# A graph-attention kernel whose rounds finish the last batch's softmax, weighing and sums ahead of the new batch's rows

## What is computed

```python
q, k, v = projections of the nodes                      # [3125, 8, 16]
e = edge_attr @ We                                      # second layer only, 64 -> 128
logits = sum(q[dst] * (k[src] + e), -1) / 4             # [53125, 8]
m = segment_max(logits, dst); ex = exp(logits - m[dst])
alpha = ex / segment_sum(ex, dst)[dst]
agg = segment_sum(alpha[..., None] * (v[src] + e), dst) # [3125, 128]
x = residual and norms and a 128 -> 512 -> 128 gelu network of agg
```

## Time and profile before

| what | value |
| --- | --- |
| median of 3 runs | 1341.0 us (1340.02 to 1342.21) |
| the profiled execution | 1341.56 us, span 1339.8 us |
| mean granted clock of TensorE | 0.796 of full speed |
| busy share of the span | DVE 77%, POOL 75%, PE 65%, ACT 56% |
| gathers of the first layer | 52.85 to 583 us |
| gathers of the second layer | 697.5 to 1224 us |
| transfers | 280.52 MB, 209 GB/s over the span |

### The profile page before, as it was taken

One profiled execution on the slowest core, in us unless ns is written; L12 is line 12 of the kernel. 1 busy time (PEld: TensorE's weight loads), 2 busy tenths in 40 slices (PEclk: granted clock), 3 DMA queues, 4 the chain that ended last, 5 costly groups with the idle time before them and its releaser, 6 DMA issues. The chain is left out here.

```text
span 1339.8 us, 25090 instructions
## 1 busy us (share of the span) xinstructions
PE 877.0 (65%) x5107; PEld 768.1 (57%) x5107; DVE 1030.4 (77%) x2702; ACT 747.1 (56%) x2535; POOL 1001.0 (75%) x1840
## 2 busy tenths in 40 slices
PE   3535666466456565558996586676676677776784
PEld 1335555455455565557875476665565565666673
DVE  4747878778668677796665888988988888899676
ACT  3314675574664655655540464665655755656775
POOL 4688888888888888832348888888888888884254
PEclk9756777777786766778997787887887887878798
DMA  7679877677777777750147788888888888885001
GB/s 200 184 205 284 243 238 247 217 241 240 221 243 231 220 246 230 228 174 3 55 123 232 250 257 273 253 255 281 245 258 268 250 268 270 262 254 175 1 1 49
DMA packets 227727, 280.52 MB, mean 209 GB/s; under 512 B 48262, under 2 KB 176420, under 8 KB 224119
## 3 DMA queue, kind: packets, MB, share of 16 engines
q1 hardware_dynamic: 185808, 167.97, 40.2%
q0 software_dynamic: 39936, 109.11, 27.2%
q10 hardware_dynamic: 1830, 1.86, 0.6%
HBM read 239.72 MB, written 39.08 MB: 208 GB/s over the span
## 5 line engine op out<-in xcount | busy, mean ns | idle before, releaser
L548 POOL DMA_INDIRECT KV<-kv_table,idx x832 | 803.7, 966 | 167.4 <-issue 154.7
L847 PE MATMUL PS<-QW,OHT 128*128 128x128 f32 x1664 | 304.7, 342 | 170.1 <-DVE PR L1146 148.9
L847 PEld LDWEIGHTS PS<-QW,OHT 128*128 128x128 f32 x1664 | 274.0, 248 | 191.3 <-issue 187.2
L675 ACT ACTIVATE AGG<-AGG,PC,RCS x800 | 309.2, 387 | 2.2 <-ACT AGG L671 1.5
L892 PE MATMUL PS<-OH,KV 128*128 128x128 f32 x1600 | 234.2, 301 | 25.4 <-ACT AGG L675 22.4
L892 PEld LDWEIGHTS PS<-OH,KV 128*128 128x128 f32 x1600 | 218.0, 215 | 38.9 <-issue 35.7
L1146 DVE TENSOR_TENSOR PR<-KV,PS 128x512 f32<-128x512 f32 x208 | 140.4, 675 | 119.1 <-DMA KV<-kv_table,idx 117.3
L671 ACT ACTIVATE AGG<-PS 128x127 f32 x800 | 208.7, 261 | 1.0 <-issue 0.9
L1139 DVE TENSOR_TENSOR KV<-KV,PS 128x1024 f32<-128x1024 f32 x104 | 125.4, 1206 | 70.5 <-DMA KV<-kv_table,idx 58.3
L667 ACT ACTIVATE PC<-PS 128x4 f32<-128x4 f32 x200 | 33.8, 169 | 233.4 <-PE PS L892 199.1
L867 PE MATMUL PS<-ident,AL 128*128 128x128 f32 x52 | 24.4, 468 | 198.2 <-DVE AL L1233 198.2
(11 more groups left out here) (163 smaller groups left out, 1330.7 us busy)
## 6 DMA issues: line engine op xcount, KB each, us to landing
QW<-q_table SPq DMA_DIRECT2D x832, 64.0 KB
REL<-rel_dram SPq DMA_DIRECT2D x52, 512.0 KB
window_dram<-OH SPq DMA_DIRECT2D x25, 1024.0 KB
OH<-window_dram SPq DMA_DIRECT2D x50, 512.0 KB, 7.2
KV<-kv_table,idx POOLq DMA_INDIRECT x832
EA<-in_edge_batch SPq DMA_DIRECT2D x52, 256.0 KB, 3.3
kv_table<-KV SPq DMA_DIRECT2D x24, 256.0 KB, 2.2
q_table<-KV SPq DMA_DIRECT2D x24, 128.0 KB, 2.2
```

Of the source, the lines that this page charges most:

```text
L548: g.indirect_dma_start(KV[:, s, j, :], None, kv_table, bass.IndirectOffsetOnAxis(ap=idx[:, s, j:j + 1], axis=0)).then_inc(gathered[s][hh], 16)
L675: sc.activation(AGG[:, ds(at, 1)], AGG[:, ds(at, 1)], ACT.Identity, bias=PC[:, m:m + 1], scale=RCS[:, n % SLOTS, j:j + 1]).then_inc(S["act ...
L847: last = te.matmul(o, OHT[:, q // 2, e0:e0 + P], QW[:, n % 2, 4 * q + m, :], start=True, stop=True)
```

## The change

Round n now does, on every engine, softmax and weighing of batch n - 1 and its sums, and the rows of batch n. On DVE the softmax of n - 1 comes whole, then `one_hots1(n + 1)`, then the four weighings, then the rows of n without anything between them. On ACT `one_hots(n + 1)` comes last, behind the four quarters of sums of n - 1. On PE the sums' last two quarters stand behind the queries and edge parts of the second half of n. There are G + 1 rounds. SP loads or stores the windows of n one round earlier, and the numbers of `FIRST_PACE` are lower. The work itself, in instructions and bytes, is the same.

```diff
-FIRST_PACE = ((2, 3), (4, 6), (7, 8))
+FIRST_PACE = ((2, 3), (4, 4), (6, 7))
...
-            f(0, soft=False, sums=False)
-            f(1, sums=False)
-            for n in range(2, G - 1):
+            f(0, sums=False)
+            for n in range(1, G):
                 f(n)
-            f(G - 1, more=False)
-            f(G, logits=False, more=False)
-            f(G + 1, logits=False, soft=False, more=False)
+            f(G, logits=False)
...
 (SP)
+                    if n:
+                        row_gates(n)
+                    if l and n == G - 1:
+                        load_last_windows()
                     if l and n + 1 < G:
                         features(n + 1, 0)
+                    if l and n < G - 1:
+                        load_windows(n, 0)
                     if l and n + 1 < G:
                         features(n + 1, 1)
+                    if l and n < G - 1:
+                        load_windows(n, 1)
                     if n + 2 < G:
                         places(n + 2)
                         load_queries(n + 2)
+                    if l == 0:
+                        store_windows(n)
...
 (ACT)
                     if sums:
                         exponentials(n - 1)
                     if logits:
                         gates_of(n)
                     if sums:
                         scale_at_d(n - 1)
                     if n == G:
                         warm(ACT.Gelu)
+                    if sums:
+                        for q in range(4):
+                            if n == G:
+                                add_up_last(q)
+                            else:
+                                add_up(n - 1, q)
+                    if n + 1 < G:
+                        one_hots(n + 1)
...
 (PE)
                     if sums:
                         turn_logits(n - 1)
                     if logits:
+                        queries_of(n, 0)
+                        queries_of(n, 1)
+                        if l:
+                            edge_part(n, 0)
+                            edge_part(n, 1)
+                    if sums:
+                        turn_alpha(n - 1)
+                        spread_gains(n - 1)
+                        add_up(n - 1, 0)
+                        add_up(n - 1, 1)
+                    if n == G:
+                        attention(*quads[0])
+                    if logits:
                         queries_of(n, 2)
+                        if l:
+                            edge_part(n, 2)
                     if sums:
+                        add_up(n - 1, 2)
...
                     if logits:
                         queries_of(n, 3)
+                        if l:
+                            edge_part(n, 3)
                     if sums:
+                        add_up(n - 1, 3)
...
 (DVE)
+                    if sums:
+                        if l == 0 and n < G:
+                            windows(n - 1, 0)
                         forward_max(n - 1)
                         turn_max(n - 1)
                         backward_max(n - 1)
                         carry_max(n - 1)
+                        max_back(n - 1)
+                        shifts(n - 1)
+                        if l == 0 and n < G:
+                            windows(n - 1, 1)
+                        segment_sums(n - 1)
+                        turn_sums(n - 1)
+                        totals(n - 1)
+                        carry_sum(n - 1)
+                        sums_back(n - 1)
+                        alphas(n - 1)
+                        gains(n - 1)
+                        next(places, None)
+                        for q in range(4):
+                            weigh(n - 1, q)
                     if logits:
+                        add_edges(n, 0)
+                        products(n, 0)
                         add_edges(n, 1)
                         add_products(n, 0)
                         products(n, 1)
                         add_products(n, 1)
...
                         add_edges(n, 2)
                         products(n, 2)
+                        add_edges(n, 3)
                         add_products(n, 2)
                         products(n, 3)
                         add_products(n, 3)
+                    else:
+                        add_first_nodes()
```

More of the change, by code:

```diff
@@ L462, in _ @@
                     round(n)
-                if l == 0:
-                    store_windows(G - 1)
             full = N // P
@@ L709, in gates_of, with round @@
                     sc.activation(GF[:, n % SLOTS, :], FIRST[:, ds(n * P, P)], ACT.Identity, bias=minus_big[:, 0:1], scale=BIG)                        .then_inc(S["ga_ready"], 1)
-                def round(n, logits=True, soft=True, sums=True, more=True):
-                    if n == G + 1:
-                        for q in range(4):
-                            add_up_last(q)
-                        return
+                def round(n, logits=True, sums=True):
                     if sums:
-                        add_up(n - 2, 0)
-                        add_up(n - 2, 1)
-                    if soft:
                         exponentials(n - 1)
@@ L723, in round @@
                     if sums:
-                        add_up(n - 2, 2)
-                    if sums:
-                        add_up(n - 2, 3)
-                    if more:
-                        one_hots(n + 1)
-                    if soft:
                         scale_at_d(n - 1)
@@ L916, in attention, with round @@
                     last.then_inc(S["att_ready"], w)
-                def round(n, logits=True, soft=True, sums=True, more=True):
+                def round(n, logits=True, sums=True):
                     if sums:
-                        add_up(n - 2, 0)
-                    if sums:
-                        add_up(n - 2, 1)
-                    if n == G + 1:
-                        attention(*quads[0])
-                        add_up(n - 2, 2)
-                        attention(*quads[1])
-                        add_up(n - 2, 3)
-                        return
-                    if n == G:
@@ L953, in round @@
-                    if logits and n < G - 1:
-                        turn_logits(n)
-                queries_of(0, 0)
-                queries_of(0, 1)
-                if l:
-                    edge_part(0, 0)
-                    edge_part(0, 1)
+                        add_up(n - 1, 3)
                 written_out(round)
@@ L1258, in weigh, with round @@
                     v.tensor_tensor(v4, v4, at, ALU.mult).then_inc(S["pv_ready"], 1)
-                def round(n, logits=True, soft=True, sums=True, more=True):
-                    if n == G - 1:
-                        last_logits()
-                        return
-                    if n == G + 1:
-                        add_first_nodes()
-                        return
-                    if logits:
-                        add_edges(n, 0)
-                    if soft:
+                def round(n, logits=True, sums=True):
+                    places = one_hots1(n + 1) if n + 1 < G else iter(())
+                    if sums:
+                        if l == 0 and n < G:
+                            windows(n - 1, 0)
                         forward_max(n - 1)
-                    if logits:
-                        products(n, 0)
-                    if soft:
                         turn_max(n - 1)
@@ L1276, in round @@
                         carry_max(n - 1)
+                        max_back(n - 1)
[12 more added lines that the diff above has]
+                            weigh(n - 1, q)
                     if logits:
+                        add_edges(n, 0)
+                        products(n, 0)
                         add_edges(n, 1)
                         add_products(n, 0)
-                    if soft:
-                        max_back(n - 1)
-                    if logits:
                         products(n, 1)
-                    if soft:
-                        shifts(n - 1)
-                    if logits:
                         add_products(n, 1)
-                    places = one_hots1(n + 1) if more else iter(())
                     next(places, None)
+                    if l == 0 and n == G - 1:
+                        windows(n, 0)
+                        windows(n, 1)
                     if logits:
@@ L1305, in round @@
                         products(n, 3)
-                    if soft:
-                        sums_back(n - 1)
-                    if soft and l == 0 and n < G:
-                        windows(n - 1, 0)
-                    if soft:
-                        alphas(n - 1)
-                        gains(n - 1)
-                    if soft and l == 0 and n < G:
-                        windows(n - 1, 1)
-                    if logits:
-                        add_products(n, 3)
-                    if soft:
-                        for q in range(4):
-                            weigh(n - 1, q)
```

78 lines of the change are left out of this document (2 added, 76 removed).

## The result

The changed kernel takes 1364.35 us (median of 4 runs, 1363.66 to 1368.14), the kernel before 1341.61 us in the same session (4 runs, 1340.02 to 1345.07). The ratio is 1.0177 with a 95% interval of 1.0162 to 1.0193, so the change costs 22.7 us. The prediction was 1354, slower, with a range that reaches to 1385. The profiled execution took 1364.29 us.

The account below looks back on a forecast made before the run. POOL's gathers bound both layers; the second layer's loop through the places, 21.55 us, would exceed their 20.27. 1341.56 + 20.6 - 7.7 = 1354.5, so about 1354 us; range 1329 to 1385, likeliest case 1344 to 1376.

Parts of the forecast that it names:

- What bounds before: POOL's queue of gathers sets the pace of both layers, 20.4 and 20.27 us a batch.
- the other side: Rival: gathers stay the bound in the second layer, places landing in under 4.0 us or PE never late; 1327, chance 0.30.
- The loop through the places: Weighing waits for the previous weighing through ACT's one-hots, SP, the places' transfer and DVE's one-hots; 19.2 and 21.55 us.
- 13.9 + 0.1 + 4.4 + 0.8 = 19.2 us: First layer's loop: ACT, SP, transfer of places, DVE's one-hots and handover; under 20.4, so the gathers keep the pace.
- ACT's 13.9 us: First layer, weighing to end of ACT's one-hots: 2.3 until sums start plus 11.6, with 0.3 added for the address load.
- the indices wait for a landed batch anyway, which hides it: On SP, indices queued behind window stores that now wait for DVE a round later; taken to cost nothing.
- The lag of the first rounds: In the rival that the first layer falls too: DVE's early lag, some 7 us, stays and grows; 1372, chance 0.07.
- 15.4 + 0.1 + 5.25 + 0.8 = 21.55 us: Second layer's loop: ACT, SP, transfer of places, DVE's one-hots and handover; over the gathers' 20.27, likeliest case, chance 0.45.
- 4.34 + 3.7: Second layer, third quarter of sums on PE: first product done, then queries, edges and sums; put at 8.3 us.
- 20.6 - 7.7 = 12.9 us: Net loss: 20.6 us lost in the second layer, 7.7 us won behind the first layer's last gather.
- The signs that were named: Profile signs: gathers 1.27 us apart, one-hots idle for REL, weighings 21 to 22 and 20.4, POOL waiting, last weighing near 595.
- The middle between 7.2 and 3.3 us: Second layer's transfer of the places, 512 KB, taken between the windows' and the features' landings: 5.25 us.

Follow-up runs that it names:

- all_three: Changed kernel with DVE's one-hots back behind the weighing, ACT's address loads before the sums, and eight gate loads at the end of SP's round 1; 1326.79 us, ratio 0.9893.
- late_places: Changed kernel with DVE's one-hots moved back behind the weighing, into the rows of the next batch; 1346.05 us, ratio 1.0030.
- split_places: Changed kernel with the transfer of the places cut in two, so DVE's half need not wait for ACT; 1356.09 us, ratio 1.0102.
- calm_start: Changed kernel with a larger first gate load, the eight remaining in pairs over SP's rounds 2 to 5, late weights in round 7; 1356.41 us, ratio 1.0115.
- gates_spread: Changed kernel with the eight remaining gate loads split three, three and two at the ends of SP's rounds 0, 1 and 2; 1362.14 us, ratio 1.0148.
- old_pace: Changed kernel with FIRST_PACE as in the kernel before; 1368.85 us, ratio 1.0179.
- early_addresses: Changed kernel with ACT loading all 16 node offsets behind the exponential and gates, before waiting for the sums; 1343.82 us, ratio 1.0008.
- two: Changed kernel with late_places and early_addresses together, gate loads not moved; 1330.9 us, ratio 0.9911.
- store_early: Changed kernel with the first layer's window store issued by SP before the places and queries; 1405.71 us, ratio 1.0456.

## Why the prediction was right in sign and range, and where it was wrong

**What bounds before, and the other side.** Right. A reordering can win only behind the gathers; that rival's price, 1327, is what all_three measures, though with two edits that the rival did not have in mind.

**The loop through the places, as a mechanism.** Right: in the second layer opening it (late_places, split_places) takes 7.5 to 9.6 us away and the waits with it. In 14 of 22 rounds there the places are the last wait in front of the weighing, in the other 8 ACT's exponential.

**The first layer: "13.9 + 0.1 + 4.4 + 0.8 = 19.2 us, under 20.4; the gathers keep the pace."** This step failed, and the first layer lost 20.2 us instead of winning 7.7. The term that was too small is ACT's 13.9 us, which is 15.9: the sums start at 2.87, not 2.3, and from there to the end of the one-hots are 12.99 us, not 11.6, mostly because the load of the addresses, taken at 0.3, leaves 1.46 us idle under the windows' store. With 15.9 + 0.1 + 4.1 + 0.8 = 20.9 the prediction's own formula gives the measured round, but it is not this loop that mostly holds it: split_places opened it, and the round stayed at 20.84. The prediction asked for 1.2 us more to turn this layer over; it got 1.7.

**Loops that were not listed.** ACT makes its one-hots ahead of the next exponential, and 4.9 us of softmax follow it to the weighing: 15.9 + 4.9 = 20.8. At the prediction's 13.9 it would have been 18.8 and harmless, so its absence is not what failed, but it is why loosening the places alone (split_places) brings this layer nothing. The loop through SP's queries and the store of the windows was not listed either; "the indices wait for a landed batch anyway, which hides it" looks at what stands behind the store and not at DVE, which waits for it. It is 20.3 us in the changed kernel and did no harm there.

**The lag of the first rounds.** It stood in a rival, at some 7 us and a chance of 0.07. By the prediction's own steps batch 2 could be weighed at 113.7 + 1.85 + 2.6 + 0.55 + 6.3 + 0.3 = 125.3 (its last gather ends at 113.7); it was at 144.34, 19 us late. Then 21 rounds add 0.52 each, 10.9, and the last two, without one-hots to make, give 3.5 back (20.19 and 17.13 us against 2 x 20.4): 26.5 us. Measured against all_three it is 621.08 - 594.06 = 27.0. So by this reckoning about seven tenths of the distance from the gathers' bound is the old late start, which a loop over the gathers' pace can't work off, and the rest is the loop's own excess. Two runs bear on that share: calm_start, in which 8.4 of 12.0 us came through to the last weighing, and gates_spread, in which all of 2.85 did. Both are gone with a loop of 19.4 us, as all_three shows.

**The second layer: "15.4 + 0.1 + 5.25 + 0.8 = 21.55 us."** Right in kind, too long in size. Measured are 20.7. One round by the timelines of DVE, ACT, SP and DVE:

```profile
1024.09 1.28 DVE L1235 TENSOR_TENSOR KV<-KV,PS 128x512 f32<-128x512 f32 x2
...
1037.54 1.15 ACT L648 ACTIVATE OHT<-OHT,one_col 128x1024 f32<-128x1024 f32 x1
...
1038.77 0.33 SPq L351 DMA_DIRECT2D REL<-rel_dram  x1
...
1044.15 0.75 DVE L1105 TENSOR_SCALAR OHT<-REL,iota_part 128x1024 f32<-128x1024 bf16 x1 [0.86 <-DMA REL<-rel_dram]
1044.82 1.28 DVE L1235 TENSOR_TENSOR KV<-KV,PS 128x512 f32<-128x512 f32 x2
```

ACT takes 14.6 here (14.9 on average, with 15.4 forecast), the places 5.4 in this round and often less: 4.5 in old_pace, against 5.25. Of ACT's terms one was added wrongly, 4.34 + 3.7 being 8.0 and not 8.3; it changes little, as 15.4 was a choice between 13.9 and 16.5. That choice supposed PE at the faster level of its clock; the granted mean between 760 and 1215 us was 0.86 of full speed. 23 rounds at 0.85 us less are 19 us, nearly all that separates the 21.6 us forecast for this stretch from the 2.8 found. The other terms held: first weighing 34.6 us behind the first gather (34.3 forecast), the last two rounds 19.07 and 19.17 (19.15).

**The sum.** Two sizes were wrong in opposite directions, +2.0 us a round in the first layer and -0.85 in the second. 20.6 - 7.7 = 12.9 us were forecast as the net loss of the profiled execution, 22.7 found. In all: the first layer came out 27.9 us worse than forecast, the second 18.8 us better. That the time fell into the range, 10 us from the likeliest value, is in good part luck. The sign and the range came out right; the place did not.

**The signs that were named.** Two came: the second layer's gathers stayed 1.26 us apart, and DVE idled before that layer's one-hots. The others did not: weighings 20.7 us apart there and not 21 to 22, 20.9 in the first layer and not 20.4, POOL hardly waiting for sums (1.0 us in five waits over the whole span), the first layer's last weighing at 621 and not near 595.

**The windows' landing.** The middle between 7.2 and 3.3 us was taken for the places. The windows themselves land in 5.4 us now, the features in 4.1; why was not tried:

```profile
OH<-window_dram SPq DMA_DIRECT2D x50, 512.0 KB, 5.4
...
EA<-in_edge_batch SPq DMA_DIRECT2D x52, 256.0 KB, 4.1
```

The places themselves took at most 4.1 and 4.5 us in the two rounds of the first layer shown above, 5.4 in the one of the second, and 7.3 behind the early store.

The rule that the prediction cites from the Trainium skill ("DMA: Bandwidth & Descriptors", "Anatomy of one DMA") gives an estimated 3.2 us for them. The section states it for transfers that GpSimd issues; the places are issued by SP. No traced landing of 512 KB here is that short (the shortest is 3.45 us, in gates_spread), so the trace does not agree with it under this load.

**Left open.** Why the runs of early_addresses scatter, and which part of the burst between 90 and 130 us makes the row of gates late, beyond that it does so with the eight loads at the head of SP's round 1 and at its end. How much of the rounds of late_places and early_addresses the store of the windows takes, since no edit moved it alone without touching the places.

## What to carry to other kernels

When a reordering brings a producer and its consumer into one round, list every loop from a weighing to the next one, through each engine's list and through each transfer, and compare all with the pace that now hides them: here two loops nearly tied at 20.9 us against 20.4, and opening the one through the places alone showed nothing in that layer. A third, over two rounds, stood at 20.3 and came forward when the first two were shortened. A lag from the first rounds is free only as long as every loop is shorter than the pace-setter; half a microsecond too much turns it into time. Move small work (an address load of 0.55 us, one-hots of 0.74) to where its engine waits anyway: 1.5 and 0.4 us a round here were the difference between 1.8% slower and 0.9% faster (two).

## What the runs showed of the hardware that was not expected

ACT's load of 8 addresses takes 0.55 us, but up to 2.2 us while the 1 MB store of the windows is in flight; with the load or the store moved, the longest between 125 and 600 us was 0.56. The same 512 KB transfer of places landed in 4.1 us (median, first layer of old_pace, which issues in the changed kernel's order) and in 7.3 us when a 1 MB store had been issued 1.4 us earlier (store_early). A row of 17 KB behind eight loads of 176 KB came some 14 us after its issue (104.06 to 117.94), and moving the eight to the end of that round only chose which row.
